# Two-layer graph network: where VectorE forms the attention's logits and sends them to DRAM

## The reference

```python
h   = relu(layernorm(x))
feats = einsum('nf,hfu->hnu', h, W)               # 8 heads x 64 units
e_self, e_neigh = feats . a_self, feats . a_neigh # the logits, per head and node
dense = leaky_relu(e_self[:, :, None] + e_neigh[:, None, :], 0.2)
att = softmax(dense where adj, else -1e10)
x   = x + relu(att @ feats + b)                   # x1 in the kernel

h   = relu(layernorm(x))
def conv(v, W, b):                                # H = (adj != 0), w = adj's first row
    return D^-1 * H @ (B^-1 * (H^T @ (v @ W^T))) + b
y   = conv(layernorm(relu(conv(h, W1, b1))) * gamma + beta, W2, b2)
x   = x + (y + h)
```

## Time and profile before

| | us |
|---|---|
| timed runs, median of 3 | 2465.8 (2464.04 to 2466.67) |
| the profiled execution | 2477.38 |
| its span, first to last instruction | 2473.8 |
| TensorE, matmuls busy | 2405.0 (97%) |
| TensorE, weight loads busy | 2056.3 (83%) |
| VectorE busy | 2040.6 (82%) |
| ScalarE busy | 1691.9 (68%) |
| GpSimd busy | 1366.3 (55%) |

### The profile page before, as it was taken

One profiled execution on the slowest core, in us unless ns is written; L12 is line 12 of the kernel. 1 busy time (PEld: TensorE's weight loads), 2 busy tenths in 40 slices (PEclk: granted clock), 3 DMA queues, 4 the chain that ended last, 5 costly groups with the idle time before them and its releaser, 6 DMA issues. The chain is left out here.

```text
span 2473.8 us, 50029 instructions
## 1 busy us (share of the span) xinstructions
PE 2405.0 (97%) x13492; PEld 2056.3 (83%) x13492; DVE 2040.6 (82%) x4501; ACT 1691.9 (68%) x4489; POOL 1366.3 (55%) x1549
## 2 busy tenths in 40 slices
PE   5799999999999999999999999999999999999997
PEld 3688888888888888888888888888888888888886
DVE  3888888888888888888888888888888888888884
ACT  2676777776766766766776776777777677676774
POOL 2365565555555556555556556556556555555553
PEclk8899999999999999999999999999999999999999
DMA  6455555555555555555555555555555555555542
GB/s 216 116 165 174 162 167 171 161 168 169 159 173 168 158 174 167 158 174 169 157 170 171 159 167 168 166 167 168 166 164 169 168 162 167 168 163 168 169 138 90
DMA packets 494608, 405.34 MB, mean 164 GB/s; under 512 B 310648, under 2 KB 392568, under 8 KB 494584
## 3 DMA queue, kind: packets, MB, share of 16 engines
q1 hardware_dynamic: 474072, 367.30, 48.9%
q10 hardware_dynamic: 20512, 37.76, 4.5%
HBM read 268.58 MB, written 136.35 MB: 164 GB/s over the span
## 5 line engine op out<-in xcount | busy, mean ns | idle before, releaser
L351 POOL TENSOR_TENSOR u<-u,mask 128x1024 f32<-128x1024 f32 x128 | 304.4, 2378 | 762.0 <-DMA u<-en_rows 762.0
L451 ACT ACTIVATE att<-u,shifts 128x128 f32<-128x128 f32 x1024 | 402.4, 393 | 220.4 <-DVE shifts L754 220.4
L874 PE MATMUL p_w1a<-W_hi,rT_hi 128*128 128x512 f32 x1024 | 416.0, 406 | 0.7 <-ACT rT_hi L574 0.7
L875 PE MATMUL p_w1a<-W_lo,rT_hi 128*128 128x512 f32 x1024 | 405.2, 396 | 0.0
L452 ACT ACTIVATE att_low<-u,shifts 128x128 f32<-128x128 f32 x1024 | 400.1, 391 | 0.0
L745 DVE TENSOR_REDUCE neg_max<-u 128x8 f32<-128x1024 f32 x128 | 156.1, 1219 | 173.5 <-POOL u L351 173.5
L879 PE MATMUL p_w1a<-W_hi,rT_lo 128*128 128x512 f32 x1024 | 259.7, 396 | 0.0
L405 POOL TENSOR_TENSOR z_lo<-raw,z_hi 128x512 fp32r<-128x512 f32 x128 | 165.2, 1291 | 150.1 <-ACT z_hi L560 150.1
L879 PEld LDWEIGHTS p_w1a<-W_hi,rT_lo 128*128 128x128 f32 x1024 | 192.4, 188 | 46.5
L560 ACT ACTIVATE z_hi<-raw 128x512 fp32r<-128x512 f32 x128 | 81.3, 635 | 216.4 <-DVE raw L811 216.4
L874 PEld LDWEIGHTS p_w1a<-W_hi,rT_hi 128*128 128x128 f32 x1024 | 193.4, 189 | 41.5 <-ACT rT_hi L574 1.2
(11 more groups left out here) (124 smaller groups left out, 6872.4 us busy)
## 6 DMA issues: line engine op xcount, KB each, us to landing
u<-en_rows SPq DMA_DIRECT2D x130, 576.0 KB, 3.9
r_blocks<-raw SPq DMA_DIRECT2D x128, 512.0 KB, 2.6
raw<-r_blocks SPq DMA_DIRECT2D x512, 128.0 KB, 2.8
xT_in<-in_xT SPq DMA_DIRECT2D x128, 256.0 KB, 3.4
att_blocks<-attB SPq DMA_DIRECT2D x128, 256.0 KB, 2.0
attT<-att_blocks SPq DMA_DIRECT2D x512, 64.0 KB, 3.0
out<-raw SPq DMA_DIRECT2D x128, 256.0 KB, 2.1
x_in<-in_x ACTq DMA_DIRECT2D x124, 256.0 KB, 3.4
```

Source lines behind the costliest of these rows:

```text
L351: nc.gpsimd.tensor_tensor(u[:, g.slot(2), 0:HEADS, :], u[:, g.slot(2), 0:HEADS, :], mask[:, :].unsqueeze(1).broadcast_to([P, HEADS, N]), A ...
L451: nc.scalar.activation(att[:, i, :], u[:, g.slot(2), i, :], ACT.Exp, bias=shifts[:, 0, i:i + 1])
L874: mm(dst, hi, w_hi, start=first, stop=False)
L875: mm(dst, hi, w_lo, start=False, stop=False)
```

## The change

1. TensorE: block 3's first half (`features(3, 0)`) moves ahead of L981, so the logits are complete there; the last of its matmuls signals a new semaphore `s_logits`. Behind L981 the second halves of blocks 2 and 3 are left.
2. VectorE: x's statistics, the two logit instructions, the aggregate and the transpose to eT now stand right behind z at the end of turn t, for graphs t+5 and t+3, where they stood at its end and at the beginning of the next turn. The attention's block transpose and hg_lo stand behind them. The logits wait for `s_logits` instead of `s_feats`. Both halves of feats open the next turn, together.
3. SyncE: en_rows goes out ahead of att_blocks; u stays behind both.
4. ScalarE: the load of x moves from behind the exponentials of heads 0 to 3 to behind the third head's.

```diff
--- before
+++ after
@@ -179,7 +179,7 @@
         s_stats0, s_mv0, s_ve0, s_rs0, s_xc = (sem("s_" + n) for n in ("stats0", "mv0", "ve0", "rs0", "xc"))
-        s_h0_hi, s_h0_lo, s_feats, s_feats_sb = (sem("s_" + n) for n in ("h0_hi", "h0_lo", "feats", "feats_sb"))
+        s_h0_hi, s_h0_lo, s_logits, s_feats, s_feats_sb = (sem("s_" + n) for n in ("h0_hi", "h0_lo", "logits", "feats", "feats_sb"))
         s_e_blk, s_es_low, s_eT, s_en_out, s_en_bc, s_u = (sem("s_" + n) for n in ("e_blk", "es_low", "eT", "en_out", "en_bc", "u"))
@@ -273,14 +273,16 @@
                     load_adj(t.plus(5))
+                if g.within(NG + 2):
+
+                    sp.wait_ge(s_eT, g.count())
+                    sp.dma_start(en_rows.rearrange("h (q a) -> q h a", a=32), eT[:, :]).then_inc(s_en_out, 16)
                 if t.plus(1).within(NG):
...
-                    sp.wait_ge(s_eT, g.count())
-                    sp.dma_start(en_rows.rearrange("h (q a) -> q h a", a=32), eT[:, :]).then_inc(s_en_out, 16)
                     sp.wait_ge(s_en_out, g.count(per=16))
@@ -441,6 +443,13 @@
+            def load_x(g):
+
+                if g.within(NG) and (g.loop is not None or g.base >= 4):
+                    act.wait_ge(s_x1, g.count(4))
+                    n = g.base if g.loop is None else g.loop * UNROLL + g.base
+                    act.dma_start(x_in[:, g.slot(4), :], x[bass.ds(n, 1), :, :].rearrange("a p d -> p (a d)")).then_inc(s_in[g.slot(4)], 16)
+
             def exps(g, half):
@@ -451,6 +460,8 @@
                                                 scale=SLOPE)
+                    if i == 2:
+                        load_x(g.plus(3))
                 last.then_inc(s_exp, 1)
@@ -534,12 +545,6 @@
                     exps(t.plus(2), 0)
-                g = t.plus(5)
-                if g.within(NG) and (g.loop is not None or g.base >= 4):
-
-                    act.wait_ge(s_x1, g.count(4))
-                    n = g.base if g.loop is None else g.loop * UNROLL + g.base
-                    act.dma_start(x_in[:, g.slot(4), :], x[bass.ds(n, 1), :, :].rearrange("a p d -> p (a d)")).then_inc(s_in[g.slot(4)], 16)
                 g = t.plus(1)
@@ -635,34 +640,10 @@
                         dve.wait_ge(s_small, SMALL * 16)
-                    if g.has(1):
-                        dve.wait_ge(s_eT, g.plus(2).count(1))
-                        dve.wait_ge(s_shifts, g.count(1))
-                    dve.wait_ge(s_rs0, g.count())
-                    scale = rs0[:, g.slot(4):g.slot(4) + 1]
-                    nc.vector.tensor_scalar(e_blk[:, 0:2 * SELF].rearrange("p (a n) -> p a n", a=2)[:, :, 0:HEADS],
-                                            p_fa[:, D2:D2 + EW].rearrange("p (a h) -> p a h", a=2), scale, None,
-                                            ALU.mult).then_inc(s_e_blk, 1)
-                    nc.vector.tensor_scalar(e_blk[:, SELF + HEADS:SELF + EW], p_fa[:, D2 + HEADS:D2 + EW], scale, SLOPE,
-                                            ALU.mult, ALU.mult).then_inc(s_es_low, 1)
                     if g.has(2):
                         dve.wait_ge(s_o, g.count(2))
+                    scale = rs0[:, g.slot(4):g.slot(4) + 1]
                     feats_of(g, 0, scale)
-                m = t.plus(4)
-                if m.within(NG + 2):
-                    if g.within(NG):
-                        dve.wait_ge(s_e_blk, g.count())
-                        dve.wait_ge(s_es_low, g.count())
-                    if m.within(NG):
-                        dve.wait_ge(s_mv0, m.count())
-                    if m.has(1):
-                        dve.wait_ge(s_en_bc, m.count(1, per=16))
-                    if m.has(2):
-                        dve.wait_ge(s_xc, m.count(2))
-                    if g.has(2):
-                        dve.wait_ge(s_exp, g.count(2, per=2))
-                    nc.vector.transpose(eT[:, :], e_blk[:, :]).then_inc(s_eT, 1)
-                if g.within(NG):
                     feats_of(g, 1, scale)
@@ -810,6 +791,47 @@
                                                    ALU.mult, ALU.add).then_inc(s_z, 1)
+                g = t.plus(5)
+                if g.within(NG):
+
+                    dve.wait_ge(s_in[g.slot(4)], g.uses(4, 32))
+                    nc.vector.bn_stats(st0[:, :], x_in[:, g.slot(4), :]).then_inc(s_stats0, 1)
+                g = t.plus(3)
+                if g.within(NG):
+
+                    dve.wait_ge(s_logits, g.count())
+                    if g.has(1):
+                        dve.wait_ge(s_eT, g.plus(2).count(1))
+                        dve.wait_ge(s_shifts, g.count(1))
+                    dve.wait_ge(s_rs0, g.count())
+                    scale = rs0[:, g.slot(4):g.slot(4) + 1]
+                    nc.vector.tensor_scalar(e_blk[:, 0:2 * SELF].rearrange("p (a n) -> p a n", a=2)[:, :, 0:HEADS],
+                                            p_fa[:, D2:D2 + EW].rearrange("p (a h) -> p a h", a=2), scale, None,
+                                            ALU.mult).then_inc(s_e_blk, 1)
+                m = t.plus(5)
+                if m.within(NG):
+                    dve.wait_ge(s_stats0, m.count())
+                    if m.has(1):
+                        dve.wait_ge(s_ve0, m.count(1))
+                        dve.wait_ge(s_eT, m.count(1))
+                if g.within(NG):
+                    nc.vector.tensor_scalar(e_blk[:, SELF + HEADS:SELF + EW], p_fa[:, D2 + HEADS:D2 + EW], scale, SLOPE,
+                                            ALU.mult, ALU.mult).then_inc(s_es_low, 1)
+                if m.within(NG):
+                    nc.vector.bn_aggr(mv0, st0[:, :]).then_inc(s_mv0, 1)
+                if m.within(NG + 2):
+                    if g.within(NG):
+                        dve.wait_ge(s_e_blk, g.count())
+                        dve.wait_ge(s_es_low, g.count())
+                    if m.within(NG):
+                        dve.wait_ge(s_mv0, m.count())
+                    if m.has(1):
+                        dve.wait_ge(s_en_bc, m.count(1, per=16))
+                    if m.has(2):
+                        dve.wait_ge(s_xc, m.count(2))
+                    if g.has(2):
+                        dve.wait_ge(s_exp, g.count(2, per=2))
+                    nc.vector.transpose(eT[:, :], e_blk[:, :]).then_inc(s_eT, 1)
                 g = t.plus(2)
@@ -817,20 +839,9 @@
                     nc.vector.transpose(attB[:, :], att[:, 0:HH, :].rearrange("p h n -> p (h n)")).then_inc(s_attB, 1)
-                g = t.plus(5)
-                if g.within(NG):
-
-                    dve.wait_ge(s_in[g.slot(4)], g.uses(4, 32))
-                    nc.vector.bn_stats(st0[:, :], x_in[:, g.slot(4), :]).then_inc(s_stats0, 1)
-                    dve.wait_ge(s_stats0, g.count())
-                    if g.has(1):
-                        dve.wait_ge(s_ve0, g.count(1))
-                        dve.wait_ge(s_eT, g.count(1))
                 if t.plus(1).within(NG):
...
                     nc.vector.tensor_tensor(hg_lo[:, :], p_w1b[:, :], hg_hi[:, :], ALU.subtract).then_inc(s_hg_lo, 1)
-                if g.within(NG):
-                    nc.vector.bn_aggr(mv0, st0[:, :]).then_inc(s_mv0, 1)
@@ -970,6 +981,7 @@
                     features(2, 0)
+                    features(3, 0).then_inc(s_logits, 1)
                 g = t.plus(1)
@@ -984,7 +996,6 @@
                     features(2, 1)
-                    features(3, 0)
                     features(3, 1).then_inc(s_feats, 1)
```

## The result

| us | before | after |
|---|---|---|
| median of 20 runs | 2466.4 (2464.04 to 2468.44) | 2492.18 (2456.01 to 2527.64) |
| the profiled execution | 2477.38 | 2505.44 |
| its span | 2473.8 | 2503.6 |
| mean granted clock | 0.991 | 0.976 |
| TensorE, matmuls busy | 2405.0 | 2406.6 |

The changed kernel is slower by the medians, 2492.18 / 2466.4 = 1.010, where 2418 was forecast. Its own executions lie 72 us apart, those of before 4 us. The comparison that leaves out runs over 1.5% above the fastest, here half of the changed kernel's, gives 1.0053 with a 95% interval of 1.0035 to 1.0071; since the spread turns out to be the kernel's own, the median of all runs is the better number.

A forecast was written before the change was run, and what follows sets the result against it. A dependency ring through every queue, 18.62 us a turn against TensorE's unheld 18.17, was taken as the bound. Turns of 18.21 save 119 x 0.41 us, less 0.5: 48 us off 2465.8, 2418 us, range 2407 to 2446.

The forecast's parts named there:

- The ring, and eT earlier: A dependency loop through every queue, 18.62 us long, sets the turn; eT comes 2.3 us sooner, 1.5 of it behind z.
- The first hold goes: TensorE's 0.30 us hold ahead of L981 goes; its operand is ready with a margin of 1.6 us.
- The second hold: TensorE's 0.25 us hold between L981 and L874: needs 1.71 of 1.75 us, margin 0.04; 0.04 us a turn taken as remaining.
- The rival that a part comes back there: At L874 hg_hi is 0.2 us late each turn, so half the gain returns: 2441 us; chance 0.18.
- hg_lo later: VectorE's hg_lo, now behind eT and the block transpose, ends at 1215.2; TensorE asks at 1216.1, a margin of 0.9 us.
- u behind attB: On SyncE's queue u follows the attention's blocks more closely and may land up to 0.6 us later; 0.8 us spare covers it.
- eT waits for the aggregate: On VectorE eT waits for the aggregate, now right ahead of it, some 0.1 us.
- x_in's load: ScalarE's load of x, now inside the exponentials, costs nothing or up to 0.1 us of ScalarE.
- the slower rival: A late x_in delays VectorE's statistics and hg_lo; at a 6.0 us landing in each turn, 2502 us; chance 0.07.
- The start: The second eT, ahead of W0's rounding, waits for the first u: 0 to 2.3 us lost, 1.5 taken.
- u and the maximum: GpSimd's addition ends 2.3 us sooner, near 1203.8; VectorE's maximum moves 1.52 us up, 0.8 us of the gain spare.
- The sum: Whole kernel: 119 turns 0.41 us shorter each, less 0.5 for start and end, 48 us off: 2418 us.

The follow-up runs named there:

- the first experiment: The changed kernel with one wait more: GpSimd's mask addition waits for VectorE's reciprocal, so it cannot start ahead of cnt; 2427.82 us, ratio 0.9849.
- the lock-free versions: The changed kernel with GpSimd's mask addition waiting for VectorE's reciprocal (2427.82 us), or with cnt split into two 128x1 instructions (2429.78 us).
- the probe: The kernel before with two tiny VectorE instructions of varying form added in each turn while GpSimd's mask addition is under way; 2471.71 us.
- forced turns: Changed kernel, cnt made to start behind GpSimd's mask addition in one turn of four, the addition waiting for the reciprocal in the others; 2597.96 us.

## Why the prediction was wrong

The forecast was 2418 us with a range of 2407 to 2446. Most of its steps hold:

- *The ring, and eT earlier.* Right. eT starts 2.0 us behind z, 1.9 by the forecast's terms (3.37 - 1.5); z starts when its matmuls end.
- *The first hold goes.* Right. L981 0.13 us behind the matmul ahead of it in the changed kernel, and the maximum waits for GpSimd in two turns of the steady part, 1.5 us in all.
- *The second hold.* Right to the hundredth: 1.75 us from L981 to L874 by the median, with a margin that was put at 0.04 us. The rival that a part comes back there did not happen.
- *hg_lo later.* Right. It ends 0.82 us ahead of its matmuls by the median; 0.9 was forecast. The experiment without TensorE's part shows what it costs when that margin is gone.
- *u behind attB.* The later landing of up to 0.6 us did not come: u lands 3.8 us after its issue by the median, 3.9 before.
- *eT waits for the aggregate* 0.32 us in 116 turns, put at 0.1. The maximum does not wait for it.
- *x_in's load.* Right that the move costs nothing, as the experiment shows. Its landing rose from 3.4 to 4.2 us, in the direction of the slower rival, and stayed short of the 5.2 us from which that would have decided. With the load in its old place it is 4.2 us as well, so the rise is not the move's.
- *The start.* The first y matmul of graph 0 is at 120.75 us in the first experiment and at 121.36 before. The start came out 0.6 us ahead by then, where 1.5 us had been taken as lost.

**The step that failed is "u and the maximum".** It moved GpSimd's addition 2.3 us up, to end at 1203.8, and asked only when its result was needed. It put at nothing what the 2.4 us of GpSimd would now lie beside. What the runs showed in its place: the addition starts 0.24 us behind VectorE's count by the median, and in 20 of 119 turns ahead of it; there the count is held to the addition's end, and the turn is 3.5 us longer. The trace of before has the sign of it. The addition would start at 1203.8 - 2.37 = 1201.43, and VectorE at that place ran:

```profile
1201.21 0.29 DVE L703 TENSOR_REDUCE G<-inc 128x1 f32<-128x128 f32 x1
1201.53 0.17 DVE L710 TENSOR_SCALAR cnt<-G 128x2 f32<-128x2 f32 x1
```

By these times the addition is 0.10 us ahead of the count. In before the addition started at 1203.70, beside the transpose of r that is the fourth instruction behind the count and has one input in SBUF. The Trainium skill states the rule: "SBUF — State Buffer", Who interferes with whom, says that VectorE and GpSimd share one pair of ports as an exclusive lock for a whole instruction, which is asked for by a tensor_scalar in its two-port mode and by an instruction with two inputs in SBUF against a GpSimd instruction that reads SBUF. By that rule the count is held until the addition ends whenever the addition is first. The trace agrees, with 20 held of 20. So does the probe: both forms with two inputs in SBUF were held, and the reciprocal with its one was not. The Trainium skill's page "VectorE: DVE Perf Modes", Mode 2×_2P, asks in SBUF for an outermost dimension, of those longer than one, that is even or, if odd, equal in source and destination. 128x2 meets that and was held; 128x1 has no such dimension and was not held.

There was a sign of it even without the page. GpSimd's G_lo takes 0.87 us in the turn around 1200 us of before (0.89 by the median), where VectorE's addition of the exponentials (L623, two inputs in SBUF, 1212.07 to 1212.75) starts ahead of it, and 0.41 us at the end, where it doesn't:

```profile
1212.15 0.87 POOL L402 TENSOR_TENSOR G_lo<-G,G_hi 128x128 fp32r<-128x128 f32 x1
...
2438.82 0.41 POOL L402 TENSOR_TENSOR G_lo<-G,G_hi 128x128 fp32r<-128x128 f32 x1
```

**A smaller step was mis-sized.** The sum took 48 us, from a profiled execution of 2477.38 us, off a median of 2465.8, "with the same turns". From profile to profile that is what the lock-free versions gave: 2473.8 - 2424.8 = 49.0 us of span. But all 20 timed executions of before ran at 2464 to 2468, so the profiled one was 11 us long by itself, and the median fell by 34.5 to 38 us only. 11 us are 0.09 us a turn: the kernel with TensorE's part alone, as fast as before, has turns of 18.54 us in its trace of a 2464.49 us run, where the profiled one of before had 18.62. 2418 was 10 us too low even with the collision away. The upper end of the range does not follow from its terms either: a hold of 0.24 us a turn leaves 0.21 x 119 = 25 us, less 2.3, which is 2443 and not 2446.

The rivals: none of the three happened as it was argued. The one with the right sign named another mechanism, x_in; the chances had 0.07 on slower, all of it there, and nothing for two engines that meet in a way they hadn't met before.

**Shown**: that the held counts are the whole loss (taken away in two ways, 2427.8 and 2429.8), which forms are held, that the load of x is neutral, and that both parts of the change are needed. **Open**: by which path SyncE's old order costs its 16.5 us, why the slower steps behind a late attention cost 1.66, 2.1 or 3.0 us in different runs, and how many counts were held in the runs that have no trace.

## What to carry to other kernels

When a change moves an operation of GpSimd in time, lay its new interval over VectorE's order. Here a tensor_scalar of 128x2 and an instruction with two inputs in SBUF that started inside GpSimd's addition were held to its end, though they had two numbers a partition to work on. Where they must meet, let the addition wait for the small one, or split it into columns: either was worth 2.5% of this kernel. This kernel scattered 3% from run to run while the one before scattered 0.2%, because two events raced for the same moment. With such a scatter, look for an instruction whose longest duration is many times its median.

## What the runs showed of the hardware

- A VectorE instruction of two numbers per partition (the tensor_scalar cnt, 128x2) lasts 2.0 to 2.4 us instead of 0.17 when a GpSimd addition of 128x1024 has started up to 0.4 us ahead of it (43 of 43 in the two traces of the changed kernel); one that started at the same moment or ahead is not touched.
- Beside the same addition a reciprocal of 128x2 and a tensor_scalar of 128x1 take 0.12 and 0.11 us; a tensor_scalar of 128x2, a tensor_tensor and a scalar_tensor_tensor from SBUF wait for its end (30 of 30 turns each).
- An idle time of 1.8 us on TensorE was followed by a granted clock of 0.54 over 3.7 us in the turn shown. Over 19 such turns the matmuls were 1.86 us late and the steps behind them cost 1.66 us more on average; over 28 forced turns 2.5 us late and 3.0 more. In 5 of the 19 turns no lower clock followed. On average the hold is paid about twice.
